# Attention and FFN kernel: a fifth strip per head for VectorE, and memory products, output and sums moved

## The reference, cut to what matters

```python
q, k, v = x @ Wq.T, x @ Wk.T, x @ Wv.T            # x is layernormed
scores = jnp.einsum('bsqhd,bthd->bqhst', qh, kh) * scale
probs = jax.nn.softmax(scores, axis=-1)
a_dot = jnp.einsum('bqhst,bthd->bsqhd', probs, vh)
a_mem = sigma_q @ memory / (sigma_q @ memory_norm)  # sigma_q = elu(q)
x = x + a_dot * (1.0 - w) + a_mem * w
x = x + x_qdq @ (weight * weight_scale).T          # x_qdq: layernormed x rounded to float8
```

## Time and profile before

| | |
|---|---|
| time, median of 3 runs | 1942.49 us (1942.41 to 1942.53) |
| the profiled execution's own time | 1942.58 us |
| its span, first to last instruction | 1940.5 us |
| mean granted TensorE clock | 1.000 of full speed |
| share of the span busy: TensorE, ScalarE, VectorE, GpSimd | 96%, 94%, 73%, 6% |

### The profile page before, as it was taken

How to read it: one execution, slowest core, us unless ns; L and a number is a source line. 1 busy time by engine, 2 the same in 40 slices (tenths; PEclk the granted TensorE clock), 3 DMA queues, 4 the chain that set the end, 5 groups by cost and what they waited for, 6 DMA issues and landing times.

```text
span 1940.5 us, 115379 instructions
## 1 busy us (share of the span) xinstructions
PE 1863.9 (96%) x54988; PEld 1162.0 (60%) x54996; DVE 1409.9 (73%) x1833; ACT 1833.6 (94%) x1596; POOL 107.2 (6%) x150
## 2 busy tenths in 40 slices
PE   8999999999999999999999999999999999999998
PEld 7885555556565555555555555555655555555555
DVE  6675777777777777787777777777777777777755
ACT  5556999999999999999999999999999999999997
POOL 5541000000000000000000000000000000000000
PEclk9999999999999999999999999999999999999999
DMA  6654111121112211222112211212112211222111
GB/s 220 201 187 153 54 54 40 45 57 45 54 41 56 78 49 42 56 58 64 47 49 56 78 47 44 57 46 76 44 53 57 78 50 41 56 50 72 43 47 46
DMA packets 131327, 130.38 MB, mean 67 GB/s; under 512 B 30451, under 2 KB 106455, under 8 KB 130855
## 3 DMA queue, kind: packets, MB, share of 16 engines
q1 hardware_dynamic: 129847, 121.15, 21.2%
q10 hardware_dynamic: 1008, 1.84, 0.3%
HBM read 86.96 MB, written 32.24 MB: 61 GB/s over the span
## 4 chain that ended last, share of the span: by engine, by line
ACT 76%; PE 21%; issue 2%; DVE 1%; POOL 0%; DMA 0%; ACTq 0%; DVEq 0%; POOLq 0%
ACT pool L865 74%; PE ps L1153 8%; PE ps L945 6%; PE ps L1028 4%; ACT pool L872 1%; PE ps L1200 1%; PE ps L918 1%; DMA resid<-in_x 0%; PE ps L984 0%; POOL q_sq L727 0%; PE ps L909 0%; POOL xn L704 0%; PE ps L926 0%; DVE v_tiles L1608 0%; DVE v_tiles L1610 0%
## 5 line engine op out<-in xcount | busy, mean ns | idle before, releaser
L865 ACT ACTIVATE pool<-ps 128x1536 f32<-128x1536 f32 (+1 forms) x1388 | 1710.1, 1413 | 17.0 <-PE ps L1028 14.7
L1153 PE MATMUL ps<-pool,v_st 64*32 64x128 f32 (+2 forms) x35744 | 1398.3, 357 | 14.7 <-issue 13.7
L1153 PEld LDWEIGHTS ps<-pool,v_st 64*32 64x32 f32 x35744 | 854.5, 106 | 210.0 <-issue 54.3
L1028 PE MATMUL ps<-q_st,k_st 51*32 51x512 f16 x16128 | 903.6, 381 | 49.0 <-ACT pool L865 11.6
L1028 PEld LDWEIGHTS ps<-q_st,k_st 51*32 51x32 f16 x16128 | 246.0, 89 | 474.3 <-ACT pool L865 427.5
L1593 DVE TENSOR_SCALAR late<-ps 128x512 int32<-128x512 f32 x248 | 171.6, 692 | 212.5 <-PE ps L1028 212.5
L1608 DVE SCALAR_TENSOR_TENSOR v_tiles<-late 128x2048 f32<-128x2048 f32 x62 | 142.1, 2293 | 148.1 <-PE ps L1153 144.7
L1612 DVE SCALAR_TENSOR_TENSOR pool<-v_tiles,late 128x2048 f32<-128x2048 f32 x62 | 142.1, 2292 | 2.1
L1610 DVE SCALAR_TENSOR_TENSOR v_tiles<-v_tiles,late 128x2048 f32<-128x2048 f32 x62 | 142.1, 2292 | 2.1
L1603 DVE SCALAR_TENSOR_TENSOR late<-late 128x2048 f32<-128x2048 f32 x62 | 141.6, 2285 | 0.0
L747 POOL TENSOR_TENSOR rstd<-var_eps,minus_half 128x1 f32<-128x1 f32 x32 | 23.0, 720 | 1696.8 <-DVE var_eps L1672 1696.8
(11 more groups left out here) (169 smaller groups left out, 955.1 us busy)
## 6 DMA issues: line engine op xcount, KB each, us to landing
v_st<-v_aug SPq DMA_DIRECT2D x64, 256.0 KB, 3.5
q_st<-q_aug SPq DMA_DIRECT2D x127, 128.0 KB
k_st<-k_aug SPq DMA_DIRECT2D x127, 128.0 KB
sigma_kept<-y_out SPq DMA_DIRECT2D x32, 256.0 KB, 2.0
q_aug<-parts SPq DMA_DIRECT2D x32, 256.0 KB, 2.7
wqT<-sigma_kept SPq DMA_DIRECT2D x32, 256.0 KB, 3.8
q_st<-q_aug SPq DMA_DIRECT2D x127, 64.0 KB
k_st<-k_aug SPq DMA_DIRECT2D x127, 64.0 KB
```

The lines of the kernel that those rows point to most:

```text
L865: act.activation(probs[:, u % HELD, 0:UNITS[u].width * CH], scored(u).rearrange("p a b -> p (a b)"), ACT.Exp, bias=LIFT, scale=EXP_UNIT / ...
L1028: return pe.matmul(ps[VW * c:VW * c + VW, bank, :], k_st[RT * r:RT * r + AUG, n % 2, keys:keys + VW], q_st[RT * r:RT * r + AUG, n % 2, q * ...
L1153: last = pe.matmul(acc[r][VW * c:VW * c + VW, :].rearrange("v (i s) -> v i s", s=VW)[:, places, :], v_st[rows, n % 2, j, :], by_place[rows ...
```

## The change

- Late strips are five in place of four (`LATE_STRIPS`: the four of the last key tile and the last one of the tile before). Both lists of units have one wide unit fewer and one narrow one more; head 0 has two more narrow units at its end.
- The late strips are weighed in three calls of 2, 2 and 1 strips (`LATE_PIECES`), from unit 15 in even heads and 13 in odd ones, where four calls of 1 began at unit 14.
- The memory products of even heads go from units 0 and 2 to units 3 and 5. The entry 9 of odd heads in `WEIGHED_LATER` is gone.
- VectorE: the last pass of the polynomial becomes `finish_late`, done in the head that uses it; intermediate values lie in `late_probs`. In even heads, the sums are taken before both memory products; in odd heads, the FFN output comes directly behind them.
- In heads whose h is not 0, the last two operations of `add_sums` run on GpSimd. `xq_now` shares its place with `k_sq`.
- The third strip of a unit changes array rows with each unit in place of each second one.

```diff
-LATE_TILE = ST - 1
-LATE = QG
+LATE_STRIPS = tuple(range(HEAD_STRIPS - QG, HEAD_STRIPS)) + (HEAD_STRIPS - QG - 1,)
+LATE = len(LATE_STRIPS)
...
-UNITS_OF_HEAD = (["2memory", "3", "2memory"] + ["3"] * 7 + ["2late"] * 4 + ["3"] * 8,
-                 ["3", "3", "2product", "3", "2spare", "3", "3"] + ["2late"] * 4 + ["3"] * 11)
+EVEN_HEAD = ["3", "3", "3", "2memory", "3", "2memory"] + ["3"] * 3 + ["2late"] * LATE + ["3"] * 8
+ODD_HEAD = ["3", "3", "2product", "3", "2spare", "3", "3"] + ["2late"] * LATE + ["3"] * 10
 WEIGH_BEHIND = 2
-WEIGHED_LATER = ((0, 1, 2), (0, 1, 2, 3, 9))
-WEIGH_LATE_AT = 14
+WEIGHED_LATER = ((0, 1, 2), (0, 1, 2, 3))
+LATE_PIECES = ((0, 2), (2, 2), (4, 1))
+WEIGH_LATE_AT = (15, 13)
...
+            for n in range(1, LAST_HEAD):
+                if n == LAST_HEAD - 1:
+                    pool_e.wait_ge(scores_ready, EXP_BASE[LAST_HEAD - 1])
+                    pool_e.memset(q_st[:, 1, :].bitcast(F32), 0.0).then_inc(last_cleared, 1)
+                    pool_e.wait_ge(last_cleared, 1)
+                if n % 2 == 0 and n >= HEADS:
+                    tile = (n - HEADS) // 2
+                    pool_e.wait_ge(f_eps, tile + 1)
+                    pool_e.tensor_tensor(rstd[:, 0, 0:1], var_eps[:, 0:1], minus_half[:, 0:1], ALU.pow).then_inc(f_rstd, 1)
+                    pool_e.wait_ge(f_rstd, tile + 1)
+                if n % HEADS != 0:
+                    add_sums(n - 1)
...
-                    last = strip_scores(THIRD_BANK[u % SLOTS], n, strip, (c // 2 + u // 2) % ROW_TILES, c)
+                    last = strip_scores(THIRD_BANK[u % SLOTS], n, strip, (c // 2 + u) % ROW_TILES, c)
...
+            def finish_late(n):
+                dve.wait_ge(late_step, n * CHAIN_STEPS)
+                dve.scalar_tensor_tensor(late_probs, late_probs, POWER[3], late_x, ALU.add, ALU.mult).then_inc(late_ready, 1)
...
             def head(n):
                 g, h = divmod(n, HEADS)
-                if n % 2 == 0:
-                    add_memory(n)
+                if n % 2 == 0 and n > 0:
+                    finish_late(n)
                 if n > 0:
                     take_sums(n - 1)
+                for unit in extras(n, "product", "weight") * (n % 2):
+                    if unit.extra == "product":
+                        ffn_out(*divmod(unit.number, TPC))
+                    else:
+                        copy_ffn_weight(unit.number)
                 if n % 2 == 0:
+                    if n > 0:
+                        dve.wait_ge(sums_added, n - 1)
+                    add_memory(n)
                     add_memory(n + 1)
+                else:
+                    finish_late(n)
                 if n > 0:
-                    add_sums(n - 1)
+                    sum_halves(n - 1)
+                    if h == 0:
+                        add_sums(n - 1)
```

More of the change, by code:

```diff
@@ L99, in extra_of, with forms_of_head @@
     return None, 0
+def forms_of_head(n):
+    if n == 0:
+        return ["2"] * EARLY_UNITS + EVEN_HEAD[:-1] + ["2", "2"]
+    return (EVEN_HEAD, ODD_HEAD)[n % 2]
 def units_of(n):
     units, strip, names = [], 0, []
-    for form in ["2"] * EARLY_UNITS * (n == 0) + UNITS_OF_HEAD[n % 2]:
+    for form in forms_of_head(n):
         width, name = int(form[0]), form[1:]
@@ L1174, in weigh_unit, with weigh_late @@
                     last.then_inc(pv_done, 1)
-            def weigh_late(n, x):
+            def weigh_late(n, piece):
+                first, strips = LATE_PIECES[piece]
                 pe.wait_ge(late_ready, n)
-                last = weigh(n, LATE_TILE, late_probs[:, x * CH:x * CH + CH], x, 1)
-                if x == LATE - 1:
+                j, q = divmod(LATE_STRIPS[first], QG)
+                last = weigh(n, j, late_probs[:, first * CH:(first + strips) * CH], q, strips)
+                if piece == len(LATE_PIECES) - 1:
                     last.then_inc(late_weighed, 1)
@@ L1233, in head @@
                         weigh_unit(weighed)
-                    x = u - EXP_BASE[n] - WEIGH_LATE_AT
-                    if n > 0 and 0 <= x < LATE:
-                        weigh_late(n, x)
+                    piece = u - EXP_BASE[n] - WEIGH_LATE_AT[n % 2]
+                    if n > 0 and 0 <= piece < len(LATE_PIECES):
+                        weigh_late(n, piece)
             def last_slot_free(i):
@@ L1619, in late_exponentials @@
                 dve.wait_ge(late_taken, n * LATE)
-                chain_begin((n - 1) * CHAIN_STEPS, LATE * CH)
-                if n == 1:
-                    for par in range(2):
-                        dve.wait_ge(v_stored[par], 16 * (NG // 2 + 1))
-                else:
+                late_powers((n - 1) * CHAIN_STEPS)
+                if n > 1:
                     dve.wait_ge(late_weighed, n - 1)
-                chain_end((n - 1) * CHAIN_STEPS, LATE * CH, late_probs).then_inc(late_ready, 1)
+                late_polynomial((n - 1) * CHAIN_STEPS)
+            def finish_late(n):
+                dve.wait_ge(late_step, n * CHAIN_STEPS)
+                dve.scalar_tensor_tensor(late_probs, late_probs, POWER[3], late_x, ALU.add, ALU.mult).then_inc(late_ready, 1)
             def take_sums(n):
@@ L1640, in add_sums @@
                 dve.reciprocal(rden[:, :, :], head_out[:, :, :, DH]).then_inc(rden_ready, 1)
+            def add_sums(n):
+                g, h = divmod(n, HEADS)
                 dve.wait_ge(rden_ready, n + 1)
@@ L1751, in head @@
                         decode_weight(h // 2)
-                for unit in extras(n, "product", "weight"):
-                    if unit.extra == "product":
+                if n == LAST_HEAD - 1:
+                    for unit in extras(n, "product"):
                         ffn_out(*divmod(unit.number, TPC))
-                    else:
-                        copy_ffn_weight(unit.number)
                 if n + 1 < LAST_HEAD:
```

46 lines of the change are left out of this document (25 added, 21 removed).

## The result

| | before | after |
|---|---|---|
| time, median of 4 runs each | 1942.51 us (1942.41 to 1944.12) | 1974.52 us (1972.16 to 1977.74) |
| ratio | 1 | 1.0164 [1.0146, 1.0182] |
| profiled execution, its span | 1942.58, 1940.5 us | 1977.74, 1976.0 us |
| granted TensorE clock | 1.000 | 0.999 |

The change costs 32 us. Predicted were 1968.6 us, range 1935 to 1982.

A forecast was written before the change was run, and what follows sets the result against it. ScalarE was taken to set the pace from unit to unit, with TensorE following. From 1942.6, less 26.0, plus 0.1, 18.6 and 33.4, came 1968.7, or 1968.6 us against the median; range 1935 to 1982.

The forecast's parts named there:

- What is taken from ScalarE: Exponentials of heads 1 to 62: one more narrow unit each saves 0.42 us a head, 26.0 us in all.
- The memory products: Units 3 and 5 of even heads: products make TensorE late, 0.60 us more in 31 heads, 18.6 us lost.
- VectorE in even heads: Units 11 and 12: TensorE waits for VectorE's first late strip, about 1.2 us in 27 heads, 33.4 us lost.
- The sums on GpSimd: Beside even heads' float8 steps: two operations of 0.64 to 1.27 us hold up VectorE, taken as 0.9 us.
- (a): Even heads' float8 steps: GpSimd's sums cost VectorE nothing, so 1950.7 us; chance 0.22 for 1946.4 to 1960.
- (e): Even heads: two whole waits of 1.27 us for GpSimd, 2.87 us in 20 heads, 2001 us; 0.08 for over 1980.
- Pieces and last pass: Late strips weighed as 2, 2 and 1, and VectorE's longer chain with its last pass: both costed at nothing.
- The third strip's rows: The other turn of the two row halves in a unit's third strip: costed at nothing.
- the first term: ScalarE's exponentials: 0.42 us saved a head by one more narrow unit, 26.0 us over 62 heads.
- the third term: Even heads, units 11 and 12: VectorE takes the first late strip too late for TensorE, 33.4 us lost.
- Rival (b): Even heads: VectorE is in time and only the memory units cost, 1935.3 us, faster; chance 0.14.
- the 26.6 that I gave as a sign: Profile after: odd heads run at about 26.6 us; wrong if even heads come near that too.

The follow-up runs named there:

- mem_early: The changed kernel with memory products back at units 0 and 2 of even heads, VectorE adding the first product ahead of the sums: 1924.76 us, 0.9914 of the kernel before.
- before_mem35: The kernel before with only the memory products moved to units 3 and 5 of even heads, sums taken ahead of both: 1969.0 us, 1.0158 of the kernel before.
- late_one_later: The changed kernel with the five late units of even heads at 10 to 14 in place of 9 to 13: 1947.1 us, 1.0021 of the kernel before.
- pool_first: The changed kernel with GpSimd's sums ahead of the power that the float8 rounding waits for, not behind it: 1966.79 us, 1.014 of the kernel before.
- weigh_at_6: The changed kernel with unit 3 of even heads weighed one unit later, at unit 6 instead of 5: 1971.67 us, 1.0181 of the kernel before.

## Why the prediction was right, step by step

- **What is taken from ScalarE, 26.0 us:** the number of narrow exponentials came out as counted (445). From head 1 to head 62, mem_early is 18.4 us shorter than before by the traces, where the medians of its heads promise 25.3 (0.32 us in an even and 0.51 in an odd head). The other 7 us are lost irregularly in single heads. Units 14 and 17 to 19 of even heads, the last three behind units that weigh late strips, lose 8.5 us there, where none of them lost 0.8 before. By the timed runs the gain is 17 to 19 us (0.9914 to 0.9902). By mem_early this term was too large by 7 to 9 us; the price that I left out is, as far as the sums by unit show, that of the units around the late pieces.
- **The memory products, 18.6 us:** the mechanism and the place were right, the size was not. In unit 5, T(6) lies 2.22 us behind T(5) and not 1.92. The step that failed is the choice of the unit that I priced it by: unit 0 of before, where TensorE had been idle 0.55 us when its scores began, and its product followed 0.34 us later (994.40 to 994.74). In unit 5 TensorE is late itself, and unit 4's weighing still runs when the scores load. The product begins 0.74 us after them (1178.66 to 1179.40), so 0.40 later, of which the rest of the unit gave 0.10 back. In the changed kernel the products' own units lose 28.5 us more than they did before (9.5 and 28.9 for 7.8 and 2.1), where the term had 18.6. before_mem35 puts the placement at 26 us by the heads of its trace (0.85 us in 31 heads) and at 31 by its timed ratio; late_one_later against mem_early gives 21 (1.0021 less 0.9914), and the 8.5 us that mem_early loses at units 14 and 17 to 19 are gone there.
- **VectorE in even heads, 33.4 us:** right, 27.8 us by late_one_later and 30.0 by the starts before unit 12. Unit 11 asked at 14.55 us from T(0) and not 14.25, since the products cost more. VectorE began its first late strip at 15.36 (1187.72), where I had VectorE free at 15.39. What was left to do for TensorE then, one late strip and the rest, took 0.27 us (1188.45 to 1188.72) and not 0.45. So T(12) was 16.36, not 16.58.
- **The sums on GpSimd:** the two operations take 0.62 and 0.71 us (0.64 to 1.27 were the bounds). They stretch two float8 steps, 0.55 to 0.88 and 0.43 to 0.80 us: 0.70 us a head where I took 0.9. The other two ways to add the sums moved the time by 8 us up and 5 us down (1.0203 and 1.014 beside 1.0164), which is near the limit of what separate groups of runs can tell. Rivals (a) and (e), which hung on it, are out: with no cost in the float8 steps (pool_first) the time is still 1.4% up, 1966.79 us where (a) had 1950.7, and (e) wanted 2.54 us a head where 0.70 stood.
- **Pieces and last pass, at nothing:** they show no cost of their own, but they carry weight. Undone one at a time, they cost 18 us (pieces, 1.0258 less 1.0164), 59 us (pieces, products early) and 29 us (last pass, products early). That cover was right for the change as it stood.
- **The third strip's rows, at nothing:** right.

In differences of the timed ratios, each times 1942.5 us: fifth strip with its helpers -17 (mem_early), products at units 3 and 5 +21 (late_one_later less mem_early), late strips met too soon +28 (after less late_one_later). They add up to the measured +32 because each starts where the last ends, so the total proves nothing, and late_one_later also has its late strips a unit later than mem_early. The prediction had -26, +19 and +33, so +26: an error of 6 us, out of two terms that were too good and one that was too bad.

Read within the changed kernel's own trace, the error lies elsewhere: odd heads fell by 0.37 us on average, close to the 0.42 of the first term, and even heads grew by 1.60 where the terms give 1.26. There the products cost 28.5 us, the late strips 30.0 and units 17 to 19 some 4. In both readings the products cost more than the 18.6 us, by 2 us in the first, which is within its noise, and by 10 in the second. That the number came so near is in part luck, since the third term was too high and made up for some of it.

Rival (b), in which only the products cost, is what late_one_later runs: 1.0021 where (b) had 0.996 (1935.3): the gain was smaller and the products cost more. The odd heads run at 27.12 us at the median and not at the 26.6 that I gave as a sign.

What stays open: why odd heads lose up to 3 us in single units 14 to 16 (TensorE's waits "issue" of up to 2.9 us stand there). It happens in every kernel here, in the one before too, and no run tested a cause. The traces do give a lead. Over all 14 of them, 29 of the 30 "issue" waits of TensorE's weight loads that last 1.8 us or more lie in heads 17, 25, 33, 41, 49 and 57. In these six the DMA moves close to 400 GB/s for 2 us, and in no other head from 1 to 61 over 272: it is 403 GB/s from 1330 to 1332 in head 41 of the changed kernel, right before its wait of 2.92 us. That this burst holds up TensorE is not shown, only that the two go together.

## What to carry to other kernels

An engine with work to spare is not enough: ask at which unit its result is wanted. Here moving two small products three units later in a head took nothing from any engine, and turned a gain of 0.9% into a loss of 1.6%, half by making one unit too full and half by making VectorE late for a bank. Where two waits follow each other in one loop, repair the later one first, since it swallows what the earlier gives back (weigh_at_6). And price a unit from one that is reached with the engine busy, not from one that it entered after a pause.

## What the runs showed of the hardware

Three things I had not expected in this size. First, VectorE's quick steps on SBUF beside a GpSimd operation. The timeline of head 34 in the changed kernel, VectorE and then GpSimd:

```profile
1127.61 0.88 DVE L1721 TENSOR_SCALAR parts<-parts,rstd,scalars 128x512 f32<-128x512 f32 x1 [0.51 <-POOL rstd L776]
1128.52 0.80 DVE L1723 TENSOR_SCALAR parts<-parts 128x512 f32<-128x512 f32 x1
1129.35 0.43 DVE L1727 TENSOR_SCALAR parts<-parts 128x512 int32<-128x512 int32 x1
```

```profile
1127.58 0.62 POOL L761 TENSOR_TENSOR head_out<-head_out,rden 128x256 f32<-128x256 f32 x1
1128.28 0.75 POOL L766 TENSOR_TENSOR resid<-resid,head_out 128x256 f32<-128x256 f32 x1
```

Each of the two VectorE steps beside them takes 0.33 and 0.37 us longer than alone, so about half of a GpSimd operation, and the third, with none beside it, takes its 0.43. These steps read one tensor each, not two; even so they are held up. With GpSimd's sums moved away from them (pool_first), the first is back at 0.55. In the earlier trace rows a tiny operation was held for a whole GpSimd operation.

Second, a product over 128 rows came later behind a busy TensorE. In unit 5 the 8 loads of scores took 0.32 us and 0.43 us of "issue" stood ahead of the product, while 29 loads of weighing over 64 rows had just gone in. In unit 3, which TensorE entered idle, it was 0.11 and 0.23 us. That the product waits for the weighing to run out fits these rows, but no run separates it from the scores ahead of it.

Third, the clock can follow a long wait. In the changed kernel TensorE stood idle for the 2.92 us in head 41; from 1335.4 to 1338.7 the granted clock was then 0.50, its lower level of 1.2 GHz, with TensorE busy throughout, and ScalarE waited a second time, 0.45 us. The same came behind the waits in heads 41 and 49 of mem_early (2.75 and 2.31 us) and in heads 33 and 49 of late_one_later (2.69 and 3.17 us), but not behind the one of 2.56 us in the kernel before. This belongs to the irregular losses, and not to the two waits that the change brought in.
